# A chain of attentions on one core: another written order of all steps, and eight products of a constant ahead of the first weights

## The reference

```python
x = L0(x, ctx)         # x + (softmax((x Wq + bq)(ctx Wk + bk)^T / 16)(ctx Wv + bv)) Wo + bo
x = L1(x, ctx, side)   # two such attentions on LayerNorm(x), keys LayerNorm(ctx) and LayerNorm(side), added to x;
                       # then x + LayerNorm(x) fc_W + fc_b
x = L2(x, ctx)         # softmax over the queries (axis 1), no Wo; LayerNorm(x + ...) * gamma + beta
x = L3(x, ctx)         # as L0
```

## Time and profile before

| what | value |
|---|---|
| median of 3 runs | 600.93 us |
| profiled execution | 600.17 us |
| its span | 598.10 us |
| TensorE busy | 574.3 us, 4712 matmuls |
| VectorE, ScalarE, GpSimd busy | 470.1, 444.9, 502.4 us |
| moved by DMA | 44.58 MB, mean 75 GB/s |
| mean granted TensorE clock | 0.985 |

### The profile page before, as it was taken

One profiled execution on the slowest core, in us unless ns is written; L12 is line 12 of the kernel. 1 busy time (PEld: TensorE's weight loads), 2 busy tenths in 40 slices (PEclk: granted clock), 3 DMA queues, 4 the chain that ended last, 5 costly groups with the idle time before them and its releaser, 6 DMA issues.

```text
span 598.1 us, 16329 instructions
## 1 busy us (share of the span) xinstructions
PE 574.3 (96%) x4712; PEld 559.4 (94%) x4712; DVE 470.1 (79%) x1470; ACT 444.9 (74%) x1520; POOL 502.4 (84%) x700
## 2 busy tenths in 40 slices
PE   4699999999999999999999999999999999999994
PEld 3699999999999999999999999999999999999973
DVE  3997698887888787788888788888877785887972
ACT  2268977777887877878976968788778898677552
POOL 4589998999899997989898598999999895776671
PEclk9799999999999999999999999999999999999997
DMA  8961211122222220222222122222121100000011
GB/s 241 359 219 45 90 45 47 47 63 80 90 72 71 81 76 33 81 81 73 63 79 68 42 81 81 71 87 76 63 81 63 38 9 19 19 3 19 19 54 54
DMA packets 30375, 44.58 MB, mean 75 GB/s; under 512 B 2768, under 2 KB 22096, under 8 KB 30288
## 3 DMA queue, kind: packets, MB, share of 16 engines
q1 hardware_dynamic: 30288, 43.54, 22.2%
HBM read 35.14 MB, written 8.39 MB: 73 GB/s over the span
## 4 chain that ended last, share of the span: by engine, by line
PE 87%; DVE 6%; issue 2%; ACT 1%; DMA 1%; SPq 1%; POOL 0%; DVEq 0%; ACTq 0%; POOLq 0%
PE bank L672 14%; PE bank L685 9%; PE bank L655 9%; PE bank L679 9%; PE bank L663 7%; PE bank L696 5%; PE bank L823 5%; PE bank L698 5%; PE bank L697 5%; PE bank L801 5%; PE bank L713 4%; PE bank L785 3%; PE bank L786 3%; PE bank L787 3%; PE bank L814 1%
## 5 line engine op out<-in xcount | busy, mean ns | idle before, releaser
L915 ACT ACTIVATE prob_L<-bank,neg_max_L 128x128 f32<-128x128 f32 x320 | 114.4, 378 | 18.5 <-DVE neg_max_L L1241 18.3
L1396 POOL TENSOR_TENSOR rstd_ln<-var_eps_ln,minus_half 128x2 f32<-128x2 f32 x64 | 45.1, 705 | 29.6 <-ACT var_eps_ln L925 29.3
L915 ACT ACTIVATION_READ_ACCUMULATOR prob_L<-bank,neg_max_L 128x1 f32 x320 | 69.4, 217 | 0.0
L1241 DVE TENSOR_REDUCE neg_max_L<-bank 128x2 f32<-128x256 f32 (+1 forms) x128 | 59.1, 476 | 11.7 <-PE bank L679 9.4
L1055 DVE TENSOR_TENSOR oT_lo_L<-bank,oT_hi_L 128x256 fp32r<-128x256 f32 (+1 forms) x96 | 48.2, 504 | 21.3 <-ACT oT_hi_L L868 20.3
L868 ACT ACTIVATE xT_hi_L<-bank 128x512 fp32r<-128x512 f32 (+1 forms) x96 | 58.4, 612 | 8.1 <-PE bank L655 5.8
L868 ACT ACTIVATE oT_hi_L<-bank 128x256 fp32r<-128x256 f32 (+1 forms) x96 | 44.9, 472 | 20.7 <-PE bank L685 19.2
L868 ACT ACTIVATE probT_L<-bank 128x256 f32<-128x256 f32 (+1 forms) x96 | 45.4, 473 | 9.0 <-PE bank L663 8.8
L1204 DVE BATCH_NORM_STATS2 stats_ln<-x 128x6 f32<-128x256 f32 x128 | 47.7, 414 | 0.9
L1055 DVE TENSOR_TENSOR xT_lo_L<-bank,xT_hi_L 128x512 fp32r<-128x512 f32 x64 | 43.6, 681 | 6.0 <-ACT xT_hi_L L868 5.3
L663 PE MATMUL bank<-ident,prob_L 128*128 128x128 f32 x256 | 43.7, 274 | 2.1 <-ACT prob_L L915 2.1
(11 more groups left out here) (225 smaller groups left out, 2351.4 us busy)
## 6 DMA issues: line engine op xcount, KB each, us to landing
x_in<-in_x SPq DMA_DIRECT2D x32, 512.0 KB, 3.5
ctx_in<-in_ctx SPq DMA_DIRECT2D x32, 256.0 KB, 3.2
out<-y SPq DMA_DIRECT2D x32, 256.0 KB, 2.2
side_in<-in_side SPq DMA_DIRECT2D x32, 128.0 KB, 2.0
WqT_L<-in_L_WqT SPq DMA_DIRECT2D x3, 256.0 KB, 4.9
Wo_L<-in_L_Wo SPq DMA_DIRECT2D x2, 256.0 KB, 5.7
WkT_L<-in_L_WkT SPq DMA_DIRECT2D x3, 128.0 KB, 5.4
WvT_L<-in_L_WvT SPq DMA_DIRECT2D x2, 128.0 KB, 5.3
```

The lines of the kernel that those rows point to most:

```text
L915: last = activation(at(prob[k], g)[:, b, :], block(bank, b), ACT.Exp, bias=at(neg_max[k], g)[:, b:b + 1], accum_out=at(total[k], g)[:, b:b ...
L1241: dve.tensor_reduce(at(neg_max[k], g)[:], scores, AX.X, ALU.max, negate=True).then_inc(done[f"max_{k}"], 1)
L1396: pool.tensor_tensor(at(rstd[k], g)[:], at(var_eps[k], g)[:], minus_half[:, 0:n], ALU.pow).then_inc(done[f"rstd_{k}"], 1)
```

## The change

`STARTS` and `PREPARATIONS` get other numbers throughout, and so every engine's program another order; no step of the computation is added or left out, and no ring changes. The last store stands at 57155 instead of 57830. A new step `first_constant` on GpSimd fills `mean_of_D`, ahead of all others, instead of the end of `constants`. A new step `run_up` on TensorE waits for it and multiplies the tile with itself eight times into the last bank, which nobody reads before it is overwritten.

The loads are now, in KB: rows_L1 128 and 128, side 0 128, cols 13, WqT_L2 256, WkT_L2 128, ctx 0 256, g2 and b2 of L1a 64 each, WvT_L1a 128, Wo_L1a 256, fc_W 256, row_fc 128, g2 and b2 of L1v 64 each, WqT_L1v 256, WkT_L1v 128, WvT_L0 128, Wo_L0 256, Wv2 128, row_L2 128, x 0 512, ctx 1 256, WqT_L0 256, WkT_L0 128, ctx 2 256, WqT_L1a 256, WkT_L1a 128, ctx 3 256, b1 and g1 of L1v 128 each, WvT_L1v 128, Wo_L1v 256, b1 and g1 of L1a 128 each, ctx 4 256, three rows of L3, ctx 5, row_L0, side 1 and 2, x 1 and 2, ctx 6 to 9.

TensorE begins with run_up, M_L2, k_L2, B2:0, n_fc, mean_fc, N_L1a, T_keys:0, n_L0, V_L2:0, N_L0, M_L0, m_L0, B2:1, V_L2:1, Q_L0:0, V_L2:2, S_L0:0, B2:2, V_L2:3, B2:3, m_L1v, M_L1v, N_L1v, PT_L0:0, B2:4, V_L2:4, O_L0:0, Q_L0:1, M_L1a. VectorE has there wk_L1a, wq_L1v, wv_L1v, bias_L0, m_col_L1v, max_L0:0, wq_L1a in this order. TensorE ends with OUT_L2:31, PT_L3:27, S_L3:28, Q_L3:29, O_L3:27, PT_L3:28, S_L3:29, O_L3:28, Q_L3:30, OUT_L3:27, PT_L3:29, T_L3:31, S_L3:30, O_L3:29, OUT_L3:28, Q_L3:31, PT_L3:30, S_L3:31, OUT_L3:29, O_L3:30, PT_L3:31, OUT_L3:30, O_L3:31, OUT_L3:31.

The diff, the tables cut to the preparations:

```diff
+RUN_UP = 8
...
-PREPARATIONS = {"M_L0": 395, "N_L0": 528, "m_L0": 484, "n_L0": 615, "M_L1a": 1381, "N_L1a": 1614, "m_L1a": 1470, "M_L1v": 2081, "N_L1v":
-    2752, "m_L1v": 2170, "n_L1": 2223, "n_fc": 1527, "mean_fc": 1702, "M_L2": 1789, "k_L2": 1876, "M_L3": 3073, "N_L3": 3166,
...
+PREPARATIONS = {"M_L0": 1491, "N_L0": 1383, "m_L0": 1579, "n_L0": 1224, "M_L1a": 2870, "N_L1a": 1093, "m_L1a": 2959, "M_L1v": 2354, "N_L1v":
+    2443, "m_L1v": 2310, "n_L1": 4589, "n_fc": 835, "mean_fc": 931, "M_L2": 508, "k_L2": 595, "M_L3": 3206, "N_L3": 3119,
...
+    1650, "load_vo_L3": 1496, "load_rows_L3": 286, "first_constant": -1000, "run_up": -1000}
...
-             "GpSimd": ["constants", "rows_L1", "rows_L3"] + ...
+             "GpSimd": ["first_constant", "constants", "rows_L1", "rows_L3"] + ...
...
+            def run_up():
+
+                prepared(pe, "first_constant")
+                for n in range(RUN_UP):
+                    mm(banks[-1][:, 0:P], mean_of_D[:], mean_of_D[:], start=True, stop=True)
...
+            def first_constant():
+                pool.memset(mean_of_D[:], 1.0 / D).then_inc(done["first_constant"], 1)
+
             def constants():
...
-                pool.memset(minus_half[:], -0.5)
-                pool.memset(mean_of_D[:], 1.0 / D).then_inc(done["constants"], 1)
+                pool.memset(minus_half[:], -0.5).then_inc(done["constants"], 1)
```

More of the change, by code:

```diff
@@ L129 @@
-    "rstd_lnf": [6165, 6878, 7975, 9516, 11340, 13053, 14882, 16700, 18083, 20003, 21672, 23322, 25156, 26676, 28416, 30453,
-        31514, 33755, 33824, 37111, 38703, 40259, 41886, 43633, 45522, 47593, 49856, 50796, 51622, 53766, 54597, 54959],
-    "lo_fc": [6461, 7105, 7862, 9372, 11197, 13084, 14826, 16531, 18251, 20088, 21621, 23284, 25005, 26528, 28428, 30353, 32133,
-        33748, 34158, 36990, 38581, 40187, 41825, 43597, 45542, 47626, 49802, 50955, 51918, 53636, 54441, 55185],
-    "OUT_fc": [6578, 7472, 8928, 9974, 11428, 13369, 15107, 16841, 18489, 20471, 21905, 23548, 25208, 26968, 29229, 30498,
-        32212, 33915, 34269, 37250, 38844, 40469, 42155, 43957, 45921, 48042, 50532, 51304, 52389, 53791, 54678, 55336],
@@ new lines @@
+    "stats_keys": [578, 2897, 3448, 3691, 4034, 4392, 6305, 7464, 8304, 9147, 10382, 13052, 14169, 16369, 17170, 18711, 21163,
+        23777, 24832, 26515, 28362, 30298, 30875, 34105, 35210, 36812, 38025, 41326, 41606, 43689, 43814, 47138],
+    "rstd_keys": [885, 3118, 3778, 4078, 4302, 6184, 7041, 8458, 8866, 9724, 12059, 14030, 15902, 16764, 18274, 20821, 23692,
[15 rows of a table added]
+    "norm_keys": [1031, 3228, 3938, 5725, 6889, 7860, 8714, 9515, 11780, 13765, 15636, 16552, 18008, 20612, 23358, 24401, 26103,
[11 rows of a table added]
@@ new lines @@
+    "T_keys": [1181, 3415, 4249, 6365, 7084, 9258, 10238, 11650, 12390, 14695, 15804, 19224, 21339, 22225, 23512, 25000, 26433,
[5 rows of a table added]
+    "t_keys": [1244, 3530, 4423, 6433, 7153, 9326, 10301, 11777, 12482, 15351, 15928, 19298, 21674, 22593, 23579, 25529, 26554,
[35 rows of a table added]
+    "T_fc": [5796, 7593, 8035, 9991, 10105, 12806, 14514, 16382, 17447, 18398, 20288, 23812, 25300, 26346, 27595, 29546, 30483,
[3 rows of a table added]
+    "hi_fc": [5886, 7700, 8121, 10102, 10539, 13056, 14578, 16450, 17612, 18512, 20354, 23876, 25482, 26459, 27687, 29610,
+        30550, 34330, 35488, 37386, 37784, 39544, 41086, 43197, 44794, 47837, 48988, 51013, 51457, 52640, 53465, 54432],
@@ new lines @@
+    "stats_lnf": [5730, 7361, 7941, 9477, 10118, 11627, 14059, 16690, 17396, 18380, 20275, 24318, 24695, 26306, 27300, 29436,
+        30772, 34360, 35457, 37330, 37674, 38288, 40814, 43346, 44032, 47264, 48098, 49182, 51157, 52420, 53329, 54347],
+    "rstd_lnf": [5990, 7685, 8263, 9655, 10421, 11920, 14254, 16863, 17584, 18567, 20544, 24541, 25050, 26700, 27564, 29656,
+        30983, 34511, 36014, 37552, 37956, 38457, 40998, 43520, 44254, 47467, 48286, 49337, 51608, 52616, 53511, 54545],
+    "lo_fc": [5971, 7763, 8184, 10222, 10626, 13178, 14652, 16554, 17692, 18575, 20445, 23939, 25571, 26640, 27808, 29742,
+        30627, 34619, 35560, 37511, 37854, 39639, 41215, 43286, 44909, 47900, 49051, 51080, 51535, 52824, 53554, 54500],
@@ new lines @@
+    "OUT_fc": [6048, 7849, 8281, 10303, 10719, 13259, 14739, 16709, 17782, 18993, 20540, 24130, 25838, 26840, 27885, 29842,
+        30712, 34961, 35640, 37622, 38020, 39716, 41330, 43407, 45004, 48042, 49132, 51294, 51639, 52901, 53633, 54614],
+    "out_fc": [6227, 8044, 8466, 10508, 10933, 13421, 14901, 16940, 17944, 19207, 20702, 24617, 26092, 27026, 28234, 30023,
[41 rows of a table added]
+    "x_res": [8000, 10702, 10965, 12954, 13286, 15273, 17163, 19010, 20155, 21221, 22466, 26437, 28311, 28752, 30461, 31904,
[17 rows of a table added]
+    "store": [9368, 12815, 13037, 15933, 16224, 18934, 21115, 22468, 23313, 23601, 24173, 27826, 30519, 30790, 32494, 33638,
[3 rows of a table added]
@@ L267 @@
                          + ["bias_L0", "bias_L1", "bias_L3", "bias_fc", "centred_fc", "F_lo", "M_lo_L2", "k_bias2", "Wv2_lo"]),
-             "GpSimd": ["constants", "rows_L1", "rows_L3"] + [f"{w}_gained_{a}" for w in ("wk", "wv") for a in ("L1a", "L1v")] + [f"rep_{a}" for a in ATTENTIONS + ["fc"]]}
+             "GpSimd": ["first_constant", "constants", "rows_L1", "rows_L3"] + [f"{w}_gained_{a}" for w in ("wk", "wv") for a in ("L1a", "L1v")] + [f"rep_{a}" for a in ATTENTIONS + ["fc"]]}
 SMALL = [f"{what}_{k}" for what in ("stats", "mean") for k in ("keys", "ln1", "lnf", "ln2")] + ["x_gamma", "zeroed", "small"]
@@ L860, in tensor_program @@
                      | {f"n_{k}": output_bias(k, LAYERS[k]) for k in LAYERS}
-                     | {"n_fc": n_fc, "mean_fc": mean_fc, "M_L2": M_L2, "k_L2": k_L2})
+                     | {"run_up": run_up, "n_fc": n_fc, "mean_fc": mean_fc, "M_L2": M_L2, "k_L2": k_L2})
         def scalar_program(act):
```

36 lines of the change are left out of this document (11 added, 25 removed), and 339 rows, old and new, of tables (PREPARATIONS, STARTS).

## The result

The changed kernel takes **604.78 us** (median of 4 runs, 604.31 to 605.17) where the kernel before takes 600.82 beside it: ratio 1.0066, 95% interval 1.0049 to 1.0083. It is slower by 0.66%, where 594.5 us (590.3 to 598.5) had been forecast. On another chip the same kernel came to 603.34 beside 601.07 (1.0042, 1.0026 to 1.0058). The profiled execution took 605.02 us, its span is 602.9; before it was 598.1.

The account below looks back on a forecast made before the run. TensorE's own work was taken to bound the middle, leaving gains at the ends: start -3.5, run-up -0.2, middle +1.0, end -3.7, sum -6.4 us, from a median of 600.93 to 594.5 us, range 590.3 to 598.5.

Parts of the forecast that it names:

- Loads and first products: First loads: bytes decide landings, M_L2 starts near 6.5 us, and the 6.6 us hole on TensorE goes.
- Start, -3.5 us: Up to M_L1a: TensorE gets through its first steps sooner, -3.5 us, bounds -5 and 0.
- wq_L1a until 34.4 to 35.6: VectorE at the start: wq_L1a, begun at 29.7, is done then, so M_L1a runs at some 35 us.
- The start is wrong if M_L1a comes after 38: Sign for the start term: M_L1a was expected at 34 to 36 us; after 38 would refute it.
- Rival 1: Start gives nothing: M_L1a comes at 39.5, only end and run-up gain, 598.0 us; chance 0.15.
- Run-up, -0.2 us: Eight unread products before M_L2 bring the clock up slightly earlier: 0.2 us gained, ends 0 and 1.5.
- Rival 2: Clock rises early: run-up and M_L2 count as one stretch, first products at full speed, 593.2 us; chance 0.12.
- Middle, +1.0 us: Middle groups: same work, thinner margins show other engines' delays on TensorE, +1.0 us, between -0.7 and +5.
- idle over 6 us: Sign for the middle: TensorE idle expected at 2 to 4 us from 40 to 565; above 6 would refute it.
- The second test named: Other sign for the middle: the term is wrong if matmuls of one shape take longer there.
- End, -3.7 us: From OUT_L2:31 to the last matmul: more work fills the last group's chain, some 17.0 us, -3.7, bounds -5.5 and -2.
- Rival 3: Slower by stalls in the middle: at 0.35 us a group, 11.2 us eat start and end, 604.7 us; chance 0.07.

Follow-up runs that it names:

- hold_both: Changed kernel with GpSimd's x_bias from group 0 on held until VectorE's wq_L1a is made: 600.30 us, ratio 0.9994 to the kernel before.
- lo_sooner: `hold_both` with VectorE, from group 4, making only 128 of 512 columns of some low parts, then an unread sum: 597.73 us, 0.9937.

## Why the prediction was wrong

*Loads and first products: right.* M_L2 at 6.33 us (forecast 6.5), no hole over 3 us from 9.8 to 23.4, and 3.8 us of lead when 18 us of work were done.

*Start, -3.5 us: wrong, +3.7.* The step that failed is "wq_L1a until 34.4 to 35.6". One preparation was priced at 4.7 us undisturbed and 5.9 beside GpSimd, from two instances of before, and 5.9 was taken for the worst. The 4.7 was a disturbed one too: its product took 1.05 us beside a GpSimd operation, and 0.69 in `hold_both`, where the whole takes 4.2. In the new order GpSimd had six operations ready at that moment, which took 1.26 us or more each, because x had landed and bias_L0 was made just before; wq_L1a began at 31.14, 1.4 us later than forecast, and took 8.05 us. "The start is wrong if M_L1a comes after 38": it came at 39.66. Rival 1 had M_L1a at 39.5 and priced that at nothing gained. It missed what follows the hole: half speed for M_L1a (2.05 us) and the steps behind it, and a lead that is not merely lost, since the light steps had already been spent ahead of the hole. With the neighbour held off, M_L1a came at 35.22, but the start still ended 1.1 us behind (0.2 ahead in `lo_sooner`, where the clock did not fall behind it). The forecast counted time up to M_L1a and took the state behind it for that of the kernel before.

*Run-up, -0.2 us: not contradicted;* no effect was measured in either order, and one of 0.2 us would not show. M_L2 ran at half speed in the changed kernel. Rival 2 did not come true: where M_L2 did run at full speed, in three other traces, the clock was at half again behind it.

*Middle, +1.0 us: right in mechanism, wrong in size; it measured +5.5* (4.4 on the second chip), where the upper bound of the term was +5. This is the second step that failed. The prediction itself read from the tables that lo_fc to OUT_fc went from 283 units to 96 and wrote that margins would become 0.3 to 0.5 us. It then priced this by the idle time of before, 1.7 us, and gave "idle over 6 us" as its test. Idle was 2.57 us; the stalls were inside the busy time, 0.0019 us per matmul or 8 us in 4371 (with the half speed behind M_L1a until 44.7, and the heavier mix). The second test named, matmuls of one shape taking longer, did show it. Its reason, that other engines' *delays* would come through, was at most part of it: more or less load left the difference of the orders about where it was, and a result 0.4 us sooner took away the waits that it touched. What makes the larger part of the 5.5 us stays open.

*End, -3.7 us: right.* 17.2 us from OUT_L2:31 to the last matmul (forecast 17.0), and -4.4 or -4.5 us by equal work in every profiled run with the changed list of TensorE (-4.7 in `lo_sooner`). One reading was off and is not in the sum: the half speed after 590 us was put at 1.1 us, where half of the 2.98 us of the earlier trace rows is 1.5.

*The rivals.* Rival 3, slower by stalls in the middle at 604.7 us, gave the right number, with a chance of 0.07. It had the start gained, though, and the middle at 11.2 us; the truth was half of that, and the start lost: the number is luck. The range failed because its upper end, 598.5, held neither the middle's worst case nor a start that loses: the start measured +3.7 where its worst bound was 0.
